# Gated cross-attention layer: keys and values as three products of split operands, fewer Newton steps, shared buffers and another order of the work

## The reference, cut to what matters

```python
# x: (32, 112, 256); ctx: (32, 375, 128); 16 heads of 16
h = layernorm(x)
q, k, v = h @ Wq + bq, ctx @ Wk + bk, ctx @ Wv + bv
o = softmax(q k^T / 4) v            # per head
x = x + tanh(g_xattn) * (o @ Wo + bo)
x = x + tanh(g_ffn) * moe_ffn(layernorm(x))
# moe_ffn: each of 8 experts takes its top 896 of the 3584 tokens by
# sigmoid(x @ Wg), applies W1 (256x1024), gelu, W2 (1024x256), scales by the gate, adds back
```

## Time and profile before

| | us |
|---|---|
| median of 3 runs | 883.53 (882.7 to 883.61) |
| the profiled execution's own time | 883.38 |
| its span, first to last instruction | 881.6 |
| PE busy | 804.9 (91% of the span) |
| DVE busy | 643.5 (73%) |
| ACT busy | 567.9 (64%) |
| POOL busy | 420.0 (48%) |

### The profile page before, as it was taken

The page is one execution under the profiler, slowest core; times in us unless marked ns, Lnnn a source line. Parts: engine busy times, 40 slices in busy tenths (PEclk is TensorE's granted clock), DMA queues, the critical chain, the costliest instruction groups (busy, mean ns, idle before and its releaser), DMA issues. The chain is left out here.

```text
span 881.6 us, 22285 instructions
## 1 busy us (share of the span) xinstructions
PE 804.9 (91%) x8336; PEld 667.1 (76%) x8336; DVE 643.5 (73%) x1548; ACT 567.9 (64%) x1251; POOL 420.0 (48%) x560
## 2 busy tenths in 40 slices
PE   5989999999999999999995119999999999999995
PEld 3555888888888888888873017979898988888885
DVE  6888888888888888888753885787676766764542
ACT  2656877787778877787663125757667574839470
POOL 4771254445544554445444503466565565744504
PEclk9999999999999999999997558999999999999998
DMA  7843676676667676667311204162535344352303
GB/s 190 197 98 86 158 169 171 158 176 161 178 156 174 162 180 159 171 160 173 108 39 37 93 0 149 43 150 49 138 57 135 86 104 118 82 136 60 41 3 42
DMA packets 96210, 104.62 MB, mean 119 GB/s; under 512 B 11744, under 2 KB 92272, under 8 KB 96112
## 3 DMA queue, kind: packets, MB, share of 16 engines
q1 hardware_dynamic: 84128, 88.50, 39.0%
q0 software_dynamic: 10752, 14.69, 9.7%
q10 hardware_dynamic: 1232, 0.12, 0.1%
HBM read 39.60 MB, written 14.68 MB: 62 GB/s over the span
## 5 line engine op out<-in xcount | busy, mean ns | idle before, releaser
L489 DVE TENSOR_REDUCE a_nm<-a_pS 112x1 f32<-112x375 f32 x342 | 177.7, 541 | 43.7 <-PE a_pS L783 40.1
L1768 PE MATMUL e_p<-w2hl,e_hh 128*128 128x512 f32 x440 | 156.9, 397 | 0.0
L777 PEld LDWEIGHTS a_pT<-a_qst,a_kst 98*128 98x128 bf16 x1536 | 105.8, 98 | 47.5 <-issue 17.5
L1562 POOL DMA_INDIRECT out_dram<-e_y,e_idx x56 | 89.1, 1592 | 109.1 <-ACT e_y L1601 102.8
L777 PE MATMUL a_pT<-a_qst,a_kst 98*128 98x112 bf16 x1536 | 133.8, 212 | 2.0 <-ACT a_room L308 0.7
L685 POOL TENSOR_TENSOR a_kp<-a_k_rest,a_kp 128x375 bf16<-128x375 f32 x56 | 49.2, 901 | 176.2 <-ACT a_kp L328 176.2
L308 ACT ACTIVATE a_P<-a_pT 128x448 f32<-128x448 f32 x192 | 99.4, 552 | 39.0 <-PE a_pT L777 38.9
L1770 PE MATMUL e_p<-w2hl,e_hl 128*128 128x256 f32 x440 | 123.1, 280 | 0.0
L1648 DVE TENSOR_TENSOR e_hl<-e_hid,e_hh 128x384 fp32r<-128x384 f32 (+1 forms) x128 | 77.9, 624 | 47.2 <-ACT e_hh L1594 46.2
L308 ACT ACTIVATE a_room<-a_pT 128x448 f32<-128x448 f32 x192 | 96.4, 539 | 19.7 <-PE a_pT L777 19.7
L489 DVE TENSOR_REDUCE a_nm<-a_pK 112x1 f32<-112x375 f32 x170 | 91.9, 540 | 21.3 <-PE a_pK L783 19.6
(11 more groups left out here) (250 smaller groups left out, 1736.8 us busy)
## 6 DMA issues: line engine op xcount, KB each, us to landing
a_kst<-a_kp SPq DMA_DIRECT2D x192, 192.0 KB, 3.3
w<-in_L_ffn_W_dram SPq DMA_DIRECT2D x16, 1024.0 KB, 7.0
a_qst<-a_qp SPq DMA_DIRECT2D x96, 112.0 KB, 3.4
a_craw<-in_ctx_dram SPq DMA_DIRECT2D x32, 128.0 KB
a_room<-in_x_dram SPq DMA_DIRECT2D x8, 448.0 KB, 6.8
a_xb<-in_x_dram SPq DMA_DIRECT2D x32, 112.0 KB, 2.1
out_dram<-a_x SPq DMA_DIRECT2D x32, 112.0 KB, 2.6
xn_scratch<-a_x SPq DMA_DIRECT2D x32, 112.0 KB, 2.8
```

What stands on the lines that cost most here:

```text
L489: dve.tensor_reduce(nm[:, h:h + 1], s_bank(b, h)[0:LQ, 0:LK], AXX, ALU.max, negate=True).then_inc(s_used, 1)
L777: last = pe.matmul(pT[u % 2][:, j * LQ:(j + 1) * LQ], kst[b % 4][:, h, c * 128:(c + 1) * 128], q_of(b, slice(None), h), start=True, stop=True)
L1562: pool.indirect_dma_start(out=out, out_offset=bass.IndirectOffsetOnAxis(ap=idx[r % 2][:, g:g + 1], axis=0), in_=y[g][:], in_offset=None, c ...
L1768: pe.matmul(p2[g % 2][:], hh[:, f, rows], T.w2hl[r % 2][:, f].rearrange("p q d -> p (q d)"), start=(f == 0), stop=(f == 7), skip_group_che ...
```

## The change

Keys (from batch 5 on) and values (from batch 5 on) become three fp32r products of split operands each: high by high, high by low, low by high. GpSimd splits the weights once, before its loop, and the context of each batch, with a copy (`context_high`) and a subtraction (`context_low`). One of the two Newton steps goes. To make room for the new tiles, `k_rest`, `O`, `cc[0]`, `ccT`, `x1`, `x2` and `x2T` lie in places of tiles that are done with by then. The order of the work in the loop is another one on every engine, the turns of bank `pM[0]` are values, cc, x2, wo, logits, and the loop ends one m earlier.

```diff
+        cTh, cTl = ([sb(f"cT{p}{i}", [128, LK2], F32R) for i in range(4)] for p in "hl")
+        wkh, wkl = (sb(f"wk{p}", [128, 2, 128], F32R) for p in "hl")
+        wvh, wvl = (sb(f"wv{p}", [128, D], F32R) for p in "hl")
...
-        FIRST, LAST, G = -2, B + 2, B // 4
-        EARLY_K, DVE_COPIES = 4, 6
+        FIRST, LAST, G = -2, B + 1, B // 4
+        EARLY_K, DVE_COPIES, EARLY_C = 4, 6, 5
...
@@ SP, in one m: after stack_keys (0, 1) and (2, 3) @@
-                if live(m + 5, 4):
-                    stack_queries((m + 5) // 2, (3, 4, 5) if (m + 5) % 2 else (0, 1, 2))
                 if live(m + 2, 1):
                     row_max(m + 2)
-                if live(m + 1):
-                    x_again(m + 1)
+                if live(m + 8, 6):
+                    context(m + 8)
                 if live(m + 4, 3):
                     stack_keys(m + 4, (4, 5))
                 if live(m - 1):
                     results(m - 1)
-                if live(m + 7, 6):
-                    context(m + 7)
+                if live(m + 1):
+                    x_again(m + 1)
+                if live(m + 6, 4):
+                    stack_queries((m + 6) // 2, (3, 4, 5) if (m + 6) % 2 else (0, 1, 2))
...
@@ POOL @@
-                for k in range(2):
-                    pool.wait_ge(root_set, 7 * b + 2 * k + 3)
-                    pool.tensor_scalar(yy[:], y[:], y[:], nvh[:], ALU.mult, ALU.mult).then_inc(root_set, 1)
...
+                pool.wait_ge(root_set, 5 * b + 3)
+                pool.tensor_scalar(yy[:], y[:], y[:], nvh[:], ALU.mult, ALU.mult).then_inc(root_set, 1)
...
+            def context_high(b):
+                pool.wait_ge(ct_copied, b + 1)
+                pool.tensor_copy(cTh[b % 4][:, 0:LK], cT[b % 4][:]).then_inc(ct_high, 1)
+
+            def context_low(b):
+                pool.wait_ge(ct_high, b - EARLY_C + 1)
+                pool.tensor_tensor(cTl[b % 4][:, 0:LK], cT[b % 4][:], cTh[b % 4][:, 0:LK].bitcast(F32), ALU.subtract).then_inc(ct_split, 1)
+
             for m in range(FIRST, LAST):
                 if live(m + 5, EARLY_K):
                     k_low_part(m + 5, 0)
+                if live(m):
+                    x2_of(m)
+                if live(m + 5, EARLY_K):
                     k_low_part(m + 5, 1)
                 if live(m + 1):
                     x_biased(m + 1)
-                if live(m):
-                    root(m)
-                    x2_of(m)
+                if live(m + 7, EARLY_C):
+                    context_high(m + 7)
+                if live(m + 1):
+                    root(m + 1)
+                if live(m + 7, EARLY_C):
+                    context_low(m + 7)
...
@@ PE, keys_at_once @@
-                pe.matmul(k_bank(b, t)[:, 0:LK], wk[:, t, :], cT[b % 4][:], start=True, stop=True).then_inc(k_ready[t], 1)
...
+                pe.wait_ge(ct_split, b - EARLY_C + 1)
+                pe.matmul(out, wkh[:, t, :], cTh[b % 4][:], start=True, stop=False)
+                pe.matmul(out, wkh[:, t, :], cTl[b % 4][:], start=False, stop=False)
+                pe.matmul(out, wkl[:, t, :], cTh[b % 4][:], start=False, stop=True).then_inc(k_ready[t], 1)
...
@@ PE, values @@
-                    last = pe.matmul(v_bank(b, nth)[0:n, c % 2 * D:(c % 2 + 1) * D], cT[b % 4][:, k0:k0 + n], wv[:],
-                                     start=True, stop=True)
...
+                    pe.matmul(out, cTh[b % 4][:, k0:k0 + n], wvh[:], start=True, stop=False)
+                    pe.matmul(out, cTh[b % 4][:, k0:k0 + n], wvl[:], start=False, stop=False)
+                    last = pe.matmul(out, cTl[b % 4][:, k0:k0 + n], wvh[:], start=False, stop=True)
```

More of the change, by code:

```diff
@@ L24 @@
 PAIRED = LK - LK % 2
+LK2 = LK + LK % 2
 KPAD = 384
@@ L401, in _ @@
                     scores(m + 1, 0)
-                if live(m):
-                    o_copy(m)
-                if live(m + 1):
                     scores(m + 1, 1)
-                if live(m - 2):
-                    logits_copy(m - 2)
+                if live(m + 2, 1):
+                    values(m + 2, 0)
                 if live(m + 1):
                     scores(m + 1, 2)
+                    scores(m + 1, 3)
                 if live(m + 5, EARLY_K):
@@ L428, in _ @@
                        .then_inc(far_exp, 1)
+                if live(m + 1):
+                    scores(m + 1, 5)
+                    scores(m + 1, 6)
+                if live(m - 1):
+                    x2t_copy(m - 1)
+                if live(m + 2, 1):
+                    values(m + 2, 1)
+                if live(m + 1):
+                    scores(m + 1, 7)
+                    scores(m + 1, 8)
+                if live(m + 5, EARLY_K):
+                    k_high_part(m + 5, 1)
                 if live(m + 2, 1):
@@ L431, in _ @@
                 if live(m + 1):
[L432 to L437, removed]
+                    scores(m + 1, 9)
+                if live(m + 6, 5):
+                    ct_copy(m + 6)
                 if live(m + 1):
-                    scores(m + 1, 9)
                     scores(m + 1, 10)
                     scores(m + 1, 11)
-                if live(m + 6, 5):
-                    ct_copy(m + 6)
                 if live(m + 5, EARLY_K):
                     k_mid_part(m + 5, 0)
+                if live(m + 1):
+                    o_copy(m + 1)
+                if live(m + 5, EARLY_K):
                     k_mid_part(m + 5, 1)
+                if live(m - 1):
+                    logits_copy(m - 1)
         @block.vector
@@ L622, in _ @@
                     score_max(m + 2, 14)
+                    score_max(m + 2, 15)
                 if live(m):
                     denominators(m)
-                if live(m + 5, EARLY_K):
-                    k_remainder(m + 5, 0)
+                if live(m + 2, 1):
+                    max_high(m + 2)
                 if live(m):
@@ L634, in _ @@
                     score_max(m + 3, 0)
+                if live(m + 5, EARLY_K):
+                    k_remainder(m + 5, 0)
+                if live(m + 3, 2):
                     score_max(m + 3, 1)
@@ L648, in _ @@
                     added(m)
+                    x1_statistics(m)
+                if live(m + 3, 2):
+                    score_max(m + 3, 7)
+                if live(m):
+                    x1_moments(m)
+                if m == B - 1:
+                    far_sigmoid_end()
         @block.gpsimd
@@ L958, in _ @@
                     scores_s(m + 2, 12)
-                if live(m - 2):
-                    logits(m, m - 2)
+                    scores_s(m + 2, 13)
+                    bank_free(m, A_PIECES, "values")
+                    values(m + 2, 0)
+                    scores_s(m + 2, 14)
                 if live(m + 1):
                     scores_t(m + 1, 2)
+                    scores_t(m + 1, 3)
                 if live(m + 2, 1):
-                    scores_s(m + 2, 13)
+                    scores_s(m + 2, 15)
+                if live(m):
+                    o_transposes(m, m)
                 if live(m + 5, EARLY_K):
@@ L987, in _ @@
                     scores_s(m + 3, 1)
+                if live(m):
+                    cc_transposes(m, m)
                 if live(m + 2, 1):
@@ L1034, in _ @@
                     weighted(m + 1, 3)
+                if live(m + 3, 1):
+                    scores_s(m + 3, 10)
+                if live(m - 1):
+                    logits(m, m - 1)
+                if live(m + 3, 1):
+                    scores_s(m + 3, 11)
 class Tiles:
```

139 lines of the change are left out of this document (68 added, 71 removed).

## The result

The changed kernel takes 889.59 us (median of 7 runs, 887.23 to 893.15), the kernel before 883.53 in the same session: a ratio of 1.0071 [1.0051, 1.0092], slower by 0.7%. The forecast was 866.0, in a range of 861 to 875. The profiled execution took 887.23, its span is 885.5 us, and the mean granted clock 0.963 against 0.961.

A forecast was written before the change was run, and what follows sets the result against it. TensorE was taken to set the loop's pace at 12.50 us, with VectorE's chain near at 12.0. Savings of 11.5 + 0.7 + 0.6 + 2.0 + 2.0 + 0.8 = 17.6 from 883.4 gave 865.8, predicted as 866.0, range 861 to 875.

The forecast's parts named there:

- GpSimd's work slows VectorE: Rival: in the loop `max_low` waits for a GpSimd subtraction, making keys1 late, 28 x 0.3 = 8 us, or 874; chance 0.06.
- m = 3 to 25: Loop iterations with both keys and values split: 23 x 0.50 = 11.5 us saved, each iteration falling to 12.00.
- m = 27, 28: Two late iterations standing at VectorE's 12.00 us; the new order brings them to 11.0, saving 2 x 1.0.
- m = 29, 30: Last two iterations, 21.1 us before; two heads moved ahead of ScalarE's exponentials and copies save 2.0 (bounds 0 and 4).
- Split: Keys and values on TensorE as fp32r products: 0.24 us less for keys, 0.26 for values, together 0.50 an iteration.
- The split gives nothing: Rival: fp32r weight loads show in part on TensorE, at 0.05 a product cancelling the gain; 878 to over 900; chance 0.06.
- Margins: Rival: hand-over margins of 0.2 us do not hold, each iteration pays 0.1 to 0.4; 869 to 877; chance 0.20.
- Splitting the products alone would run into: Claim that in the old order VectorE's chain stands at about 12.0 us, so the new order has to move it.
- GpSimd: GpSimd's work per loop iteration: 7.3 us of 12.0, with `context_high` 0.55 and `context_low` 0.90, all covered.
- SP's queue and the keys: Stacking transfers queue behind the context, land 3.3 us after issue at 14.4, wanted at 15.9; nothing paid, margin 1.5.
- slower-side rival: Keys land late: beyond 4.8 us to landing each iteration pays; at 5.5, 20 us, or 886; chance 0.08.
- The Newton step: Tail: one Newton step less on the way to the last logits saves 0.8 us, `root` falling from 2.90 to 2.1.

The follow-up runs named there:

- experiment 1: Changed kernel with the `max_high` copy of the row maxima written as a reduction over an axis of length one: 875.53 us, ratio 0.9889 to the kernel before.
- experiment 5: Kernel before with only GpSimd's order changed, low keys of half 1 moved behind `x_biased` and `root`: 905.18 us, ratio 1.0232.
- experiment 6: Changed kernel with GpSimd's order low keys 0, `x2_of`, `x_biased`, low keys 1: 892.72 us, ratio 1.0084 to the kernel before.
- experiment 2: Changed kernel with both low-keys subtractions on GpSimd ahead of `x2_of`: 873.7 us, ratio 0.9884 to the kernel before.
- experiment 3: Changed kernel with the old order, bank turns and both Newton steps, context split ahead of the low keys: 874.78 us, ratio 0.9891 to the kernel before.
- experiment 4: Changed kernel with its new order and one Newton step, but fp32 products for all batches and no context split: 886.98 us, ratio 1.0017 to the kernel before.

## Why the prediction was wrong

**The step that failed** is the one that let stand for every meeting: "in 29 cases they never took over 332 ns though `x2_of` ran beside them". That row is of `max_low` beside `x2_of`, which lets VectorE go after 0.58 us; even its three longest, 0.33 each, are waits for that moment. The low keys let it go only at their end (experiments 1, 5 and 6), and no row showed a copy or `max_low` beside them. The working had the meeting in its own numbers: `context_low` ends at 1.6, low keys 0 and `x2_of` bring GpSimd to 3.7, and the denominators end at 3.68, where `max_high` follows. The trace has both at 6.12 to 6.16 after the start of `weighted` in each of the 23 iterations (6.13 is 3.68 on the prediction's clock, whose zero lies 2.45 behind that start), since both chains hang on the same iteration. From there the rival "GpSimd's work slows VectorE" was priced for the wrong instruction (`max_low` late, `max_high` not) and at 0.3 instead of 0.70, with a chance of 0.06. Its time of 874 would have been 866 + 18 x 0.7 + 5 x 0, or 879, had it been priced by a full wait in the 18 iterations that turned out to have one. The nearest row for the bound was there: one layer-norm instruction at 1980 ns against 412 beside a filling GpSimd. I cited it and then didn't use it as the upper bound of a meeting. Beside the fill it reads:

```profile
61.22 2.65 POOL L661 MEMSET a_kst<- 2x3072 int32 x1
62.05 1.98 DVE L478 TENSOR_SCALAR a_room<-a_room,a_xmv,a_xrs 112x256 f32<-112x256 f32 x1
```

It ends 0.16 after the fill, and so do three others of that line that met one (0.53, 0.92 and 1.31 us). The wait for the end of GpSimd's instruction was in the trace of the kernel before.

The Trainium skill (GPSIMD Engine Reference, Specifications) says that GpSimd shares its SBUF interfaces with VectorE, and that VectorE's instructions with two SBUF inputs are among those that contend. The traces agree, `max_low` being such an instruction (0.40 to 0.45 against 0.175), and show that the price is not GpSimd's slowness but what stands beside it at one moment: 0.13 or 0.87 us for the same copy.

**The sum, term by term**, in the changed kernel and, without the hold, in experiment 2. All in us gained against the kernel before, from distances of `weighted`. For m = 3 to 25 that is batch 3 to batch 26; batch 3 of the kernel before, then batches 3 and 26 of experiment 2:

```profile
121.85 1.36 PE L797 MATMUL a_pO<-a_P,a_V 128*32 128x112 f32 x48
...
118.70 1.36 PE L827 MATMUL a_pO<-a_P,a_V 128*32 128x112 f32 x48
...
397.22 1.36 PE L827 MATMUL a_pO<-a_P,a_V 128*32 128x112 f32 x48
```

| Term | forecast | changed kernel | experiment 2 |
|---|---|---|---|
| m = 3 to 25 | 11.5 | -4.4 | 9.1 |
| m = 0 to 2 | 0.7 | 0.3 | 0.9 |
| m = 26 | 0.6 | 0.3 | 0.4 |
| m = 27, 28 | 2.0 | 1.4 | 1.4 |
| m = 29, 30 | 2.0 | -0.2 | -0.2 |
| sum | 16.8 | -2.6 | 11.5 |

- *Split.* Mechanism right, size off by 0.04 by its rows and 0.07 by the spacing: 0.43 in experiment 3. Weight loads hide behind neighbours, as the earlier trace rows said. "The split gives nothing" falls. (Its 0.05 a product was also misadded: 15 products make 0.75, which is more than the gain of 0.50.)
- *Margins.* The other hand-overs of the new order hold: 0.05 an iteration (experiment 4), 0.04 between experiments 2 and 3. The rival priced them at 0.1 to 0.4. VectorE's and ScalarE's own work was put too low, at 9.8 and 9.3 an iteration: the earlier trace rows give 10.3 and 9.9, and experiment 2 has 10.5 and 10.2. Nothing hung on it.
- *"Splitting the products alone would run into" VectorE at 12.0.* Not at 12.07: the old order carried the split whole. Whether it would bind just below isn't tried. The reason given for the new order was not needed.
- *GpSimd.* 80 us of 155 in the changed kernel, 85 in experiment 2, or 6.7 of 12.1 an iteration where 7.3 was said; `context_high` takes 0.50 (0.55 forecast), `context_low` 0.98 (0.9). All hidden as work; it is its place that cost.
- *SP's queue and the keys.* No wait of TensorE for a DMA of `a_kst` in 145 to 425; the median landing is 3.2 (3.3 in experiment 2), the largest 4.5. The slower-side rival that I had named was the wrong one.
- *The end.* m = 27 and 28 gained 1.4 of 2.0. m = 29 and 30 gained nothing: 21.3 in the new order, with the split or without it (21.45), 20.9 in the old order with it and 21.06 before. So two heads moved ahead of ScalarE did not shorten the last two, and the term of 2.0, taken between bounds of 0 and 4, belonged at or below its lower one.
- *The Newton step* is gone from the last root (478.90 to 480.99, 2.1 as said). From the last `weighted` to the last store's issue are 12.66 us against 13.45, so the 0.8 is there. But the next stage begins 4.1 us after that issue, where it began 2.5 after it before, and the gain is lost again: from the last `weighted` to the end of the span are 415.5 us against 414.8, and 414.1 to 418.7 over the experiments. Why that differs is open.

Together: 16.8 forecast in the stretch, 11.5 there without the hold, and the hold takes 292.02 - 278.52 = 13.5 of them in the 23 iterations, nearly 18 x 0.74. The profiled execution is 21.4 us above the forecast for it (887.2 against 865.8): 14.1 between experiment 2 and the changed kernel in the stretch, 5.3 between forecast and experiment 2 there, and 2.1 outside (the 0.8 of the tail, and 1.3 in what lies before and behind). The median of 889.59 lies 2.4 above the profiled execution.

What is shown and what isn't: that the loss comes from the copy's form (experiment 1) beside the low keys (2), that `x_biased` makes such a hold as well (6), and that split and order are innocent (3, 4, 5). What in a GpSimd instruction decides how long it holds isn't shown. The number of tensor inputs isn't it alone: a fill with none holds to its end, `x2_of` with one to 0.58 us of 1.24, low keys and `x_biased` with two to their end. Why six of 22 copies slip through isn't shown either. They are meetings in which both begin within 0.02 us, and the records don't say which engine came first; where GpSimd is clearly first, no copy slips.

## What to carry to other kernels

When two engines' chains both hang on the same iteration, put their starts on one clock and look at who stands beside whom: a GpSimd subtraction or sum of two tensors must not begin just ahead of a short copy from SBUF to SBUF on VectorE, nor of an instruction with two inputs in SBUF, where TensorE waits for what follows. A "never slow" row counts only for the partner it was taken beside, and for the moment at which it met it. If a spacing comes in two sizes, compare one iteration of each: the line that differs is the cause. The remedy can be as small as two lines exchanged on the side engine, or a reduction over one element in place of a copy.

## What the runs showed of the hardware

- VectorE's 16-column copy to bf16 takes 0.13 to 0.17 us alone. Where it begins during a GpSimd instruction with two tensor inputs, it ends with it: 0.74 (`x_biased`), 0.87 and 0.93 (low keys), 1.54 (both in a row).
- VectorE's own two-input instruction on 16 columns, `max_low`, is held in the same way: 0.40 to 0.45 in the changed kernel against 0.175, since 0.4 of GpSimd's instruction was left, and up to 1.5 beside two in a row. Copies and `max_low` end 0.02 to 0.05 us after GpSimd's instruction in 118 of 118 cases.
- Beside `x2_of` (one tensor input, 1.24 us) both wait until 0.57 to 0.60 us into it if they begin 0.13 to 0.36 us into it: 0.22 to 0.44. Beside a GpSimd fill of 2.65 us, a VectorE layer-norm instruction waited for its end: 1.98 against 0.41.
- A reduction of the same data at the same place is not held: 0.124 us in 23 of 23, and 0.13 where it began 0.17 us after GpSimd's.
- `normalise` and `added`, which read PSUM, kept their 0.41 to 0.42, and the score maxima their 0.54.
